# A mixture-of-experts kernel on one core: routing slots and shared sums ahead of the scans, a split turn of the normed rows, and routing operations with one SBUF tensor

## The reference, cut to what matters

```python
# mixing: a recurrence over time, k = layernorm(x), v = ctx; p, q, o are carried
no = max(o, u + kt); A = exp(o - no); E = exp(u + kt - no)
y  = (A * p + E * vt) / (A * q + E)
...
x = x + tanh(g_xattn[0]) * y
xf = layernorm(x)
scores = xf @ gate_w.T                      # 8 experts
ew, ei = top_k(scores, 2); ew = softmax(ew)
routed = sum over the two chosen experts of ew * expert(xf)
shared = silu(xf @ sh_gate.T) * (xf @ sh_up.T) @ sh_down.T
x = x + tanh(g_ffn[0]) * (routed + sigmoid(xf @ se_gate_w.T) * shared)
```

## Time and profile before

| what | value |
|---|---|
| median of 3 runs | 2246.73 us (2244.1 to 2248.29) |
| the profiled execution: time, span | 2253.1 us, 2251.3 us |
| mean granted TensorE clock | 0.944 of full speed |
| busy in the whole span: PE, DVE, ACT, POOL | 1968.3, 1298.9, 757.8, 864.7 us |
| 0 to 533 us (the stage of the change): PE, DVE, ACT, POOL busy | 435.18, 426.65, 159.29, 291.98 us |
| 54.02 to 460.06 us (13 turns): PE, DVE busy, granted clock | 353.00, 337.30 us, 0.93 |

### The profile page before, as it was taken

How to read it: one execution, slowest core, us unless ns; L and a number is a source line. 1 busy time by engine, 2 the same in 40 slices (tenths; PEclk the granted TensorE clock), 3 DMA queues, 4 the chain that set the end, 5 groups by cost and what they waited for, 6 DMA issues and landing times.

```text
span 2251.3 us, 38774 instructions
## 1 busy us (share of the span) xinstructions
PE 1968.3 (87%) x11898; PEld 1393.7 (62%) x11899; DVE 1298.9 (58%) x3013; ACT 757.8 (34%) x2192; POOL 864.7 (38%) x840
## 2 busy tenths in 40 slices
PE   3898888988999999469999999999999969988886
PEld 2566666665777777347777777777777754433332
DVE  6878888885644444237777767676766632222221
ACT  3323333224322222255554545454545411111110
POOL 5556655544543333142333333333333241222121
PEclk9999999999999999669999999999999989999998
DMA  7432222223333333321111111111111268999995
GB/s 257 130 85 92 77 84 84 84 90 103 104 102 101 102 102 95 135 95 67 67 67 67 67 68 66 68 67 67 67 67 67 99 259 348 404 402 407 401 410 156
DMA packets 113560, 319.47 MB, mean 142 GB/s; under 512 B 31298, under 2 KB 39490, under 8 KB 105220
## 3 DMA queue, kind: packets, MB, share of 16 engines
q1 hardware_dynamic: 86388, 264.83, 31.6%
q0 software_dynamic: 26880, 52.68, 8.2%
q10 hardware_dynamic: 144, 0.03, 0.0%
HBM read 257.33 MB, written 62.33 MB: 142 GB/s over the span
## 4 chain that ended last, share of the span: by engine, by line
PE 24%; DMA 16%; DVE 9%; issue 6%; ACT 2%; POOL 1%; DVEq 0%; SPq 0%; POOLq 0%; ACTq 0%
DMA out<-routed_ym,routed_place 15%; PE attn_ffn_ps L343 10%; PE attn_score_ps L1430 3%; PE attn_tr_ps L1443 3%; DVE attn_nmax L1744 2%; PE attn_out_ps L1457 2%; PE attn_route_ps L1475 2%; PE attn_score_ps L1433 1%; ACT attn_pr L1596 1%; PE attn_tr_ps L1400 1%; DVE attn_norm_stats L305 1%; PE attn_ffn_ps L1412 1%; DVE attn_hot L1794 1%; DVE attn_silu_gate L1832 1%; DVE attn_silu_gate L1831 1%
## 5 line engine op out<-in xcount | busy, mean ns | idle before, releaser
L1596 ACT ACTIVATE attn_pr<-attn_score_ps,attn_nmax 128x128 f32<-128x128 f32 x496 | 201.5, 418 | 203.7 <-DVE attn_nmax L1744 203.7
L1707 POOL DMA_INDIRECT list<-attn_pair,attn_pos x192 | 190.8, 994 | 65.2 <-issue 61.0
L343 PE MATMUL attn_ffn_ps<-attn_xnT_high,second_ffn_wgu_high 128*128 128x256 f32 x704 | 206.0, 293 | 8.3 <-DVE attn_hT_low L1836 8.1
L343 PE MATMUL attn_ffn_ps<-attn_xnT_low,second_ffn_wgu_high 128*128 128x256 f32 x704 | 197.4, 280 | 0.0
L343 PE MATMUL attn_ffn_ps<-attn_xnT_high,second_ffn_wgu_low 128*128 128x256 f32 x704 | 197.3, 280 | 0.0
L315 POOL TENSOR_SCALAR attn_norm_var_eps<-attn_norm_mean_var 128x2 f32<-128x2 f32 x32 | 7.9, 247 | 478.0 <-DVE attn_norm_mean_var L309 477.9
L543 PE MATMUL wkv_ffn_ps<-wkv_xnT,wkv_wg 128*128 128x256 f32 x512 | 146.2, 436 | 25.2 <-DVE wkv_x L858 24.1
L1988 POOL DMA_INDIRECT out<-routed_ym,routed_place x32 | 50.2, 1568 | 294.3 <-DMA out<-routed_ym,routed_place 263.5
L1744 DVE TENSOR_REDUCE attn_nmax<-attn_score_ps 128x2 f32<-128x256 f32 x248 | 126.4, 551 | 63.7 <-PE attn_score_ps L1433 62.8
L343 PEld LDWEIGHTS attn_ffn_ps<-attn_xnT_high,second_ffn_wgu_high 128*128 128x128 f32 x704 | 133.0, 189 | 18.9 <-DVE attn_hT_low L1836 12.2
L1030 POOL DMA_INDIRECT y<-routed_ys,first_ffn_pair x72 | 73.3, 1018 | 186.0 <-DVE routed_ys L1186 176.3
(11 more groups left out here) (286 smaller groups left out, 4803.4 us busy)
## 6 DMA issues: line engine op xcount, KB each, us to landing
second_ffn_room<-in_w_gu SPq DMA_DIRECT2D x16, 2816.0 KB, 30.7
second_ffn_more<-in_w_gu SPq DMA_DIRECT2D x16, 2816.0 KB, 31.1
second_ffn_room<-in_w_down SPq DMA_DIRECT2D x16, 1536.0 KB, 24.1
second_ffn_more<-in_w_down SPq DMA_DIRECT2D x16, 1536.0 KB, 25.1
wkv_x<-in_x SPq DMA_DIRECT2D x32, 512.0 KB, 4.0
second_ffn_room<-y SPq DMA_DIRECT2D x32, 512.0 KB, 5.6
wkv_vT<-in_ctxT SPq DMA_DIRECT2D x16, 512.0 KB, 4.3
xn<-wkv_xn SPq DMA_DIRECT2D x16, 512.0 KB, 2.8
```

The costliest lines, as they stand in the source:

```text
L343: ins = nc.tensor.matmul(out, a[i], b[j], start=start and n == 0, stop=stop and n == 2)
L1596: nc.scalar.activation(pr[u % 2][:, a, j:2 * j + 1, :].rearrange("p k t -> p (k t)"), score_ps[:, a, KEYS[j]], ACT.Exp, bias=nmax[u % 2][: ...
L1707: nc.gpsimd.indirect_dma_start(io["list1"], bass.IndirectOffsetOnAxis(ap=pos[b.s][:, j, k:k + 1], axis=0), pair[b.s][:, j, k, :], None, bo ...
```

## The change

Three edits, all in `wkv_phase`. First, VectorE does `slots(two)` and `shared(two, 0)` before `q_sums`, and `shared(two, 1)` between `denominator` and `p_sums`. Second, PE turns the normed rows one tile at a time: tile 0 before the last product of `down(two, 1)`, tile 1 behind it, and it multiplies the first gate's columns of tile 0 (`first_gate(one, 0)`) before `logits`, those of tile 1 after. Third, small operations of `route` are written with one SBUF tensor: two `tensor_scalar` for the gap in place of one `tensor_tensor`, four for the one-hot in place of one, and a `tensor_reduce` for `chosen`.

```diff
-POST_STEPS0, TABLE_STEPS0 = 24, 15
+POST_STEPS0, TABLE_STEPS0 = 23 + TJ * K0, 15
...
-                def post_xn(b):
-
-                    for j in range(TJ):
-                        pe.wait_ge(norm2.done_s, 2 * b.i + j + 1)
-                        for k in range(KC):
-                            ins = nc.tensor.transpose(blocks(post_ps[j])[:, k, :], xn[:, j, k * P:(k + 1) * P], c.ident[:])
-                        ins.then_inc(xn_tr, 1)
+                def post_xn(b, j):
+
+                    pe.wait_ge(norm2.done_s, 2 * b.i + j + 1)
+                    for k in range(KC):
+                        ins = nc.tensor.transpose(blocks(post_ps[j])[:, k, :], xn[:, j, k * P:(k + 1) * P], c.ident[:])
+                    ins.then_inc(xn_tr, 1)
+
+                def first_gate(b, j):
+
+                    pe.wait_ge(xn_ev, 2 * b.i + j + 1)
+                    if j == 0:
+                        pe.wait_ge(freed, FB0 * b.i + 1)
+                    for k in range(KC):
+                        nc.tensor.matmul(ffn_ps[0][:, j * P:(j + 1) * P], wg[:, k, 0:P], xnT[:, k, j * P:(j + 1) * P],
+                                         start=(k == 0), stop=(k == KC - 1))
...
                 def gate_up(b, n):
-                    pe.wait_ge(freed, FB0 * b.i + n + 1)
-                    for w, col in ((wg, 0), (wu, T)):
+                    if n == 0:
+                        first_gate(b, 1)
+                    else:
+                        pe.wait_ge(freed, FB0 * b.i + n + 1)
+                    for w, col in ((wg, 0), (wu, T))[n == 0:]:
...
-                def down(b, j):
+                def down(b, j, one=None):
                     pe.wait_ge(freed, 2 + FB0 * b.i + M0 - 1 + j)
                     for k in range(M0):
+                        if one and k == M0 - 1:
+                            post_xn(one, 0)
...
                     if two:
-                        for j in range(TJ):
-                            down(two, j)
+                        down(two, 0)
+                        down(two, 1, one)
                     if one:
-                        post_xn(one)
+                        if not two:
+                            post_xn(one, 0)
+                        post_xn(one, 1)
+                        first_gate(one, 0)
                         logits(one)
...
-                    v.tensor_tensor(gap[:, :, 0:1], top[:, :, 0:1], top[:, :, 1:2], ALU.subtract).then_inc(gap_s, 1)
+                    for j in range(TJ):
+                        v.tensor_scalar(gap[:, j, 0:1], top[:, j, 0:1], top[:, j, 1:2], None, ALU.subtract).then_inc(gap_s, 1)
...
-                    posts.did(v.tensor_tensor(
-                        hot[:].rearrange("p j k e -> p (j k) e"),
-                        c.expert_no[:, 0:E0].unsqueeze(1).to_broadcast([P, TJ * K0, E0]),
-                        atf[:].rearrange("p j k -> p (j k)").unsqueeze(2).to_broadcast([P, TJ * K0, E0]), ALU.is_equal))
-                    posts.need(8)
+                    for j in range(TJ):
+                        for k in range(K0):
+                            found = posts.did(v.tensor_scalar(hot[:, j, k, :], c.expert_no[:, 0:E0], atf[:, j, k:k + 1], None, ALU.is_equal))
+                    posts.need(found)
                     wait(dve, rank_s, b.i)
-                    v.tensor_tensor(chosen[:], hot[:, :, 0, :], hot[:, :, 1, :], ALU.add).then_inc(chosen_s, 1)
+                    with nc.allow_low_precision(reason="each sum is 0 or 1"):
+                        v.tensor_reduce(chosen[:], hot[:].rearrange("p j k e -> p j e k"), AX.X, ALU.add).then_inc(chosen_s, 1)
...
+                    if two:
+                        slots(two)
+                        shared(two, 0)
                     q_sums(b)
                     denominator(b)
                     if two:
-                        slots(two)
+                        shared(two, 1)
                     p_sums(b)
-                    if two:
-                        shared(two, 0)
                     bonus_values(b)
-                    if two:
-                        shared(two, 1)
```

More of the change, by code:

```diff
@@ L637, in gaps @@
                 def gaps(b):
-                    act.wait_ge(gap_s, b.i + 1)
+                    act.wait_ge(gap_s, TJ * (b.i + 1))
                     nc.scalar.activation(tgap[:], gap[:], ACT.Tanh, scale=0.5).then_inc(tgap_s, 1)
```

## The result

The changed kernel takes **2263.6 us** (median of 4, 2261.4 to 2268.4), the kernel before 2246.7 (4 runs, 2244.1 to 2248.3) on the same chip: ratio 1.0073, 95% interval 1.0044 to 1.0102. It is slower, and the forecast of 2202 was wrong.

What follows compares the result with a forecast made beforehand. A loop through VectorE and PE bounds the kernel; afterwards GpSimd sets turns of 28.1 us instead of 31.23. Together 45 us are saved: profiled 2253.1 becomes 2208, and the median, 6.4 lower, 2202 us; range 2184 to 2222.

Steps and rivals of the forecast that it cites:

- the reading of the loop: Old turn, 30.72 us: VectorE to its first shared sum (13.0), PE to the logits (5.8), VectorE to next zero (11.9).
- both orders: VectorE reordered frees the bank at 7.2 instead of 13.0; PE reordered has the logits back at about 12.6.
- if VectorE were the only bound: A turn limited by VectorE alone: 14.8 + 9.7 + 0.4 + 2.0 = 26.9 us.
- numerator` starts then: On GpSimd, after the last scatter: `numerator` starts at 17.0 to 18.3 us in the turn, 17.5 in the old one.
- the chain of scatters: GpSimd ahead of `numerator`: first scatter at 10.35, second at 12.0, ending 14.5 to 15.75, two more ending 17.0 to 18.3.
- The last norm step (the shift): GpSimd, block `after`: starts about 7.3, just behind the scan's start at 7.2, and ends with the scan at 9.5.
- The margin: In `route`: the one-hot on VectorE starts at 16.3, ahead of `numerator` on GpSimd at 17.0 to 18.3.
- Rival D: In `route`, if a microsecond late: one-hot waits for `numerator` to 19.4 to 20.7; turn 29.7 to 31.0, about 2231; chance 0.06.
- The quotient: On VectorE: wants to start at 24.9, inside GpSimd's `values`, so it starts at 25.4 to 26.7.
- Case A: GpSimd's `values` holds VectorE's quotient: turns of 27.4 to 28.7 us, result 2193 to 2209; chance 0.55.
- The routing operations: Four more VectorE instructions in `route`: 0.3 to 0.8 us more per turn, 0.4 taken, covered by the wait for `values`.
- The sum: Over the stage: 12 x 3.13 + 4.2 = 41.8 us saved, together 45 with the other turns; 2208 profiled, median 2202.

Runs made afterwards that it cites:

- kernel 5: Changed kernel with every routing operation in a form that can't be held (cast a reduce, one-hot one `tensor_tensor` with its table in PSUM): 2196.8 us.
- the order alone: The kernel before with only VectorE's new order (`slots` and `shared(two, 0)` ahead of `q_sums`): 2247.5 us, ratio 1.000.
- kernel 1: Changed kernel with one more wait on GpSimd: `numerator` waits until `route` has written `chosen`; 2202.3 us, ratio 0.979 to the kernel before.
- kernel 6: As kernel 5, but the cast is four copies of one column, SBUF to SBUF, in place of the reduce: 2197.1 us.

## Why the prediction was wrong, point by point

- **Right:** the reading of the loop and both orders. The bank is free 7.6 us after the turn's zero at 293.01 (7.2 was said), the stretch ends at 15.0 (14.8), the logits are back at 13.2 (12.6), the gate runs at full clock (1.00 from 301 to 304), and the norm shift that comes first in the turn, block `one`'s, is short again (0.20). Without the hold (kernel 5) the turn is 26.9, the very number of "if VectorE were the only bound". Some of that is luck: the 26.9 holds 0.4 for four more instructions, which kernel 5 doesn't have, and four of its turns are lengthened by a held quotient.
- **The step that failed** is in the part on GpSimd: "`numerator` starts then", at 17.0 to 18.3. It starts at 16.04, and the cast stands at 16.23. In turns 3 to 14 it is 1.0 behind the start of `route` (1.01 to 1.03) instead of 2.2 to 3.5, when the small operations were to be over. The forecast came from the chain of scatters ahead of it. The last norm step (the shift) of block `after` was to start behind the scan, at 7.3 against 7.2, and be held to 9.5. It started at 7.27, as said, but the scan began only at 7.52, and the shift took 0.20. So the first scatter started at 8.0 instead of 10.35, and the second at 10.99, ahead of the scan of `p_sums` (11.71) instead of inside it; it took 0.98, and only the first and the third were long (2.69 and 2.49). It is this second race that counts: in the sixth turn the shift is held (2.19), but the second scatter still starts 0.46 ahead of that scan, and `numerator` is 1.01 behind `route`; in the second turn the second scatter starts inside it, and `numerator` is 2.29 behind. In most turns it was decided by 0.7 us.
- **The margin would not have been enough either.** The new one-hot was to start at 16.3, 0.7 ahead of the earliest `numerator`, and its four operations take 0.63. In the second turn `numerator` stands where the forecast had it, and the third of them is held for 5.30. The old operations do slip through there (second turn of the changed kernel with old routing operations, and the turn at 330.06 of the order alone).
- **The collision was priced on the wrong operation and too low.** Rival D had the mechanism and 0.06, and let a late `route` cause it; an early `numerator` does the same. It let the one-hot wait for `numerator` only, 2.4 at most. `undrift` follows without a gap, since its inputs now lie ready, and the hold is 4.50. In the earlier trace rows `undrift` stood alone, so 2.26 was a whole hold there. That the old turn left 0.59 between the two operations (335.80 + 2.36 to 338.75), in which the routing operations slipped through, I had counted as a wait to be saved. It was the opening.
- **The quotient** was not held (1.22) in the changed kernel: `values` starts at 22.0 and ends at 24.4, and the quotient at 29.7. It is held in turns where `numerator` starts 2.3 or more behind `route` and `route` isn't held: 1.40 in the turn of kernel 1, 1.71 to 1.73 in four turns of kernel 5, 1.87 in the turn at 330.06 of the order alone. Case A's mechanism is real and worth 0.2 to 0.7, not 1.2.
- **The routing operations**: 0.4 more per turn was said. From `route` to quotient there are 14.65 against 9.72, 4.34 of it the hold (4.50 less 0.16) and 0.59 the rest.
- **The sum**: 27.48 a turn (kernel 1, all three edits, no hold) and 4.34 make 31.8; over the same twelve turns 32.3 was measured, and the late `chosen` of the result's section probably stands for the rest. So the term of the sum that was missing is the hold, 4.34 a turn. That kernel 1, the change without it, takes 2202.3 and the forecast said 2202 is luck: its last `route` starts 54.1 earlier than before and not 45, mostly since the turns are 27.48 and not 28.1, and behind it 1742.3 us remain in its profile where the kernel before had 1736.9, which the forecast took as unchanged.

The Trainium skill, "SBUF — State Buffer", Who interferes with whom, says that copy, cast and `tensor_scalar` can take both ports and then shut GpSimd out, or be shut out, for a whole instruction, and that `tensor_reduce` never does. The runs agree: 4.50 for the cast, 4.73 with the one-hot, 0.14 for the reduce. They go beyond it in that the hold spans two GpSimd instructions. "VectorE: DVE Perf Modes", Mode 2×_2P, ties that mode to SBUF on both sides and an outermost non-unit dimension that is even, or odd and equal for source and target. A copy of one column has no dimension above one in a partition, and kernel 6's (0.33 for four) were not held; that this is the reason is argued, not shown. The prediction had used the page for the quotient, and for the one-hot only under a late `route`. It never listed the cast, since no diff line touches it.

## What to carry to other kernels

When VectorE and GpSimd both work in one loop, list every VectorE operation that can be held, the unchanged ones too, and lay it against every GpSimd operation at the new times; a forecast with an uncertainty of 1 us can't say that a chain of tiny operations misses a pair of 2.36 us ones. Rather than aim for the miss, write the tiny operations so that they can't be held (a reduce, one column, an operand in PSUM), or let the GpSimd operation that has slack wait for them: a wait of 1.43 us on GpSimd (in the turn shown) brought 4.8 us a turn, 61 in all. An edit measured alone can be worth nothing for want of its partner: 0.0% and 0.2% apart, 2.7% together.

## What was unexpected of the hardware

- Two GpSimd operations back to back hold VectorE through both: 4.31 to 4.74 us for one instruction in four kernels, 2.20 where 1.09 us lay between them. VectorE had been waiting for 2.2 us when the first one ended and did not get in. A `tensor_scalar` that started 0.61 ahead of the first, during a scatter, was held through both too (5.30).
- A cast of four elements to the partition is held, a cast of one is not, nor a reduce of four, nor a `tensor_tensor` with one of its two inputs in PSUM (0.15 to 0.33 in each case, with `numerator` running).
